# Masked cross-attention: values projected on 64-column tiles, chunk 0's mask loaded straight beside its queries, VectorE's first masks and value blocks placed elsewhere, the last chunks' steps in another order

## The reference

```python
Q = split_heads(x @ w_q.T + b_q)            # x: 4 x 1024 x 256
K = split_heads(ctx @ w_k.T + b_k)          # ctx: 4 x 64 x 256
V = split_heads(ctx @ w_v.T + b_v)
scores = Q @ K.T / 4                        # 4 x 16 x 1024 x 64
scores = where(mask[:, None] == 0, -1e9, scores)
attn = softmax(scores, axis=-1)
out = merge_heads(attn @ V) @ w_o.T + b_o + x
out = (out - mean) * rsqrt(var + 1e-5) * gamma + beta
```

## Time and profile before

| | us |
|---|---|
| median of 3 runs | 165.19 (164.49 to 167.47) |
| profiled execution, its own time | 164.33 |
| its span (first to last instruction) | 162.5 |
| PE busy | 137.3 (84%) |
| DVE busy | 124.9 (77%) |
| POOL busy | 115.5 (71%) |
| ACT busy | 94.7 (58%) |

### The profile page before, as it was taken

The page is one execution under the profiler, slowest core; times in us unless marked ns, Lnnn a source line. Parts: engine busy times, 40 slices in busy tenths (PEclk is TensorE's granted clock), DMA queues, the critical chain, the costliest instruction groups (busy, mean ns, idle before and its releaser), DMA issues.

```text
span 162.5 us, 2904 instructions
## 1 busy us (share of the span) xinstructions
PE 137.3 (84%) x992; PEld 87.0 (54%) x992; DVE 124.9 (77%) x231; ACT 94.7 (58%) x166; POOL 115.5 (71%) x111
## 2 busy tenths in 40 slices
PE   0798975989899998999899989998999579999400
PEld 0676853746556655565556565655665335468300
DVE  0263899348788897989798979898989797999951
ACT  3349687593963666766676675846763815640220
POOL 5003741029999539999999999999981899667783
PEclk9999999699999999999999999999999999999955
DMA  4988983999927886006730940048003503003024
GB/s 119 342 234 198 283 197 85 317 244 269 287 71 187 314 217 252 0 0 196 180 148 0 224 167 0 2 105 274 12 2 76 187 0 129 0 4 122 7 94 166
DMA packets 10175, 23.21 MB, mean 143 GB/s; under 512 B 1584, under 2 KB 1840, under 8 KB 10160
## 3 DMA queue, kind: packets, MB, share of 16 engines
q1 hardware_dynamic: 9584, 22.03, 46.7%
q10 hardware_dynamic: 576, 0.99, 1.9%
HBM read 14.62 MB, written 4.19 MB: 116 GB/s over the span
## 4 chain that ended last, share of the span: by engine, by line
PE 45%; DVE 15%; POOL 14%; issue 7%; DMA 7%; SPq 6%; ACT 3%; POOLq 1%; DVEq 0%
PE ps_w L436 11%; PE ps_w L357 9%; PE ps_w L331 8%; DMA m_sb<-maskT 7%; PE ps_s L385 6%; PE ps_s L412 5%; POOL y L873 5%; DVE nmax L667 4%; POOL y L876 4%; DVE turned L688 3%; SPq L215 3%; PE ps_s L391 3%; ACT y L585 2%; DVE cn L701 2%; POOL rstd L857 2%
## 5 line engine op out<-in xcount | busy, mean ns | idle before, releaser
L667 DVE TENSOR_REDUCE nmax<-ps_w 128x8 f32<-128x512 f32 x56 | 37.7, 678 | 15.2 <-PE ps_w L357 14.8
L572 ACT ACTIVATE probs<-ps_s 128x512 f32<-128x512 f32 x64 | 33.1, 602 | 18.3 <-PE ps_s L396 18.3
L810 POOL TENSOR_TENSOR xt_l<-xt_sb,xt_h 128x1024 fp32r<-128x1024 f32 x7 | 16.6, 2374 | 30.6 <-ACT xt_h L533 19.8
L436 PE MATMUL ps_w<-wo_sb,cn 128*128 128x256 f32 x112 | 29.3, 387 | 3.9 <-DVE cn L701 3.6
L357 PEld LDWEIGHTS ps_w<-k_half,q_mask 128*128 128x128 f32 x112 | 17.3, 190 | 25.5 <-DVE nmax L667 19.7
L357 PE MATMUL ps_w<-k_half,q_mask 128*128 128x256 f32 x112 | 27.9, 335 | 3.2 <-DVE nmax L667 2.9
L436 PEld LDWEIGHTS ps_w<-wo_sb,cn 128*128 128x128 f32 x112 | 19.3, 189 | 9.2 <-DVE cn L701 5.5
L585 ACT ACTIVATE y<-res,shift,rstd 128x256 f32<-128x256 f32 x28 | 14.8, 590 | 12.6 <-POOL shift L859 12.5
L873 POOL TENSOR_TENSOR y<-y,brow 128x512 f32<-128x512 f32 x14 | 17.9, 1279 | 4.5 <-ACT y L585 4.1
L688 DVE STREAM_TRANSPOSE turned<-ps_s 128x1024 f32<-128x1024 f32 x16 | 19.8, 1240 | 0.8 <-PE ps_s L412 0.8
L844 POOL TENSOR_TENSOR x_sb<-x_sb,brow 128x1024 f32<-128x1024 f32 x8 | 19.1, 2382 | 0.1
(11 more groups left out here) (75 smaller groups left out, 203.3 us busy)
## 6 DMA issues: line engine op xcount, KB each, us to landing
m_sb<-maskT SPq DMA_DIRECT2D x32, 128.0 KB, 3.5
q_mask<-mask SPq DMA_DIRECT2D x32, 128.0 KB, 2.6
x_sb<-x SPq DMA_DIRECT2D x8, 512.0 KB, 4.3
xt_sb<-xT SPq DMA_DIRECT2D x7, 512.0 KB, 4.4
out<-y SPq DMA_DIRECT2D x6, 512.0 KB, 3.4
xt_sb<-xT SPq DMA_DIRECT2D x2, 256.0 KB, 5.7
out<-xt_sb SPq DMA_DIRECT2D x2, 256.0 KB, 2.0
brow<-bias_rows SPq DMA_DIRECT2D x1, 384.0 KB, 6.4
```

Source lines behind the costliest of these rows:

```text
L436: return pe.matmul(tile_outputs(c, i)[:, t], cn[:, c % 2, j, (2 * i + t) * P:(2 * i + t + 1) * P], wo_sb[:, j], start=j == 0 and c < LAST, ...
L572: act.activation(probs[:, g % 2, quad], ps_s[:, quad], ACT.Exp).then_inc(e_done, 1)
L667: dve.tensor_reduce(nmax[:, c % 2, t].rearrange("p (q r) -> p q r", r=32)[:, :, 2 * j:2 * j + 2], max_bank(c, i).rearrange("p (q h k) -> p ...
```

## The change

Six things.

1. Values: `project_values` is one function. For each batch and each part of the width it makes two matmuls, one for the even and one for the odd heads, each with 64 stationary columns (the keys of one batch) and 128 moving ones (every other group of 16 columns of wv), into rows 0 to 63 or 64 to 127. ctx_t loses its fifth block. `value_blocks` has two instructions in place of five.
2. Chunk 0's mask: SyncE loads it twice more as int32 into `m_first`, rows 0 to 63 and 64 to 127, right after xT 0, and VectorE writes its values straight into `q_mask` (`first_mask_values`). The copies of mask 0 are gone; mask 0 in its usual form is loaded later, behind xT 1 and wv, and computed after the half keys.
3. VectorE's mask 2 and the value blocks stand after the third maximum of chunk 1, no longer after the eighth of chunk 0.
4. ScalarE takes the high part of chunk 1 before the first queries leave.
5. In step 6 the eighth maximum of chunk 7 stands before the moments of chunk 5. In the tail VectorE has `divide(6, 1)` after the residual and moments of chunk 5, TensorE `values(6, 1)` after the two outputs of chunk 5.
6. GpSimd has `last_deviations(0)` before the deviations of chunk 6's second half; the counts in `deviations_done` follow.

```diff
         def deviations_done(c, second):
-            return 4 * (c + 1) if c < LAST - 2 else 4 * (LAST - 2) + 4 * (2 * (c - LAST + 2) + second + 1)
+            if c < LAST - 2:
+                return 4 * (c + 1)
+            halves = 2 * (c - LAST + 2) + second + 1
+            return 4 * (LAST - 2) + (4 * halves if halves < 4 else 18 if c < LAST else 14 + 6 * second)
@@ sync
             load_first_xt(1)
+            for half in range(2):
+                sp.dma_start(m_first[rows(half)], maskT[0]).then_inc(in_mfirst, 16)
+            load_xt(1)
+            sp.dma_start(wv_sb[:], wv).then_inc(in_wv, 16)
             load_mask(0)
-            sp.dma_start(wv_sb[:], wv).then_inc(in_wv, 16)
-            load_xt(1)
-            copy_mask(0)
             load_mask(1)
@@ tensor
+            def project_values():
+                pe.wait_ge(in_wv, 16)
+                for b in range(BATCHES):
+                    for d in range(PC):
+                        for h in range(2):
+                            mm = pe.matmul(projected_values(h)[:, b], ctx_t[:, d, b],
+                                           wv_sb[:, d].rearrange("p (q e) -> p q e", e=32)[:, :, 16 * h:16 * h + 16],
+                                           start=d == 0, stop=d == PC - 1)
+                            if d == PC - 1:
+                                mm.then_inc(v_done, 1)
@@ max_scores
                 if i == 0:
-                    pe.wait_ge(mk_in[c % 2], 16 * QUADS * (c // 2 + 1))
+                    if c == 0:
+                        pe.wait_ge(mfirst_done, 2)
+                    else:
+                        pe.wait_ge(mk_in[c % 2], 16 * QUADS * (c // 2 + c % 2))
@@ tensor's list
             project_first_queries()
-            project_values(0)
-            project_values(1)
-            project_values(2)
+            project_values()
             max_scores(0, 0)
-            project_values(3)
             max_scores(0, 1)
...
                 if s == LAST:
-                    values(LAST - 1, 1)
                     output(LAST - 2, 1, 0)
                     output(LAST - 2, 1, 1)
+                    values(LAST - 1, 1)
                     scores(LAST, 1)
@@ scalar's list
             identity_rows(0)
+            high_x(1)
             first_queries_out(0)
-            high_x(1)
             first_queries_out(1)
@@ vector
+            def first_mask_values():
+                dve.wait_ge(in_mfirst, 32)
+                for half in range(2):
+                    r = rows(1 - half)
+                    dve.tensor_scalar(q_mask[r, 0, half], m_first[r].unsqueeze(1).to_broadcast([64, 2, CHUNK]), 0.0, -BIG,
+                                      ALU.is_equal, ALU.mult).then_inc(mfirst_done, 1)
...
             first_low_x()
-            mask_values(0)
+            first_mask_values()
...
             first_half_keys()
+            mask_values(0)
             for i in range(HALVES):
                 maxima(0, i)
                 if i == 3:
                     mask_values(1)
-            mask_values(2)
-            value_blocks()
             for s in range(LAST):
...
                 maxima(front, 2)
                 if s >= 2:
                     moments(s - 2, 1)
+                elif s == 0:
+                    mask_values(2)
+                    value_blocks()
                 maxima(front, 3)
...
                 maxima(front, 6)
-                if s >= 1:
+                if front == LAST:
+                    maxima(front, 7)
                     moments(s - 1, 0)
-                maxima(front, 7)
+                else:
+                    if s >= 1:
+                        moments(s - 1, 0)
+                    maxima(front, 7)
                 divide(s, 0)
-            divide(LAST - 1, 1)
             residual(LAST - 2, 1)
             moments(LAST - 2, 1)
+            divide(LAST - 1, 1)
             divide(LAST, 0)
@@ gpsimd's tail
             affine(LAST - 1, 0)
+            last_deviations(0)
             deviations(LAST - 1, slice(2, 4))
-            last_deviations(0)
             last_deviations(1)
```

More of the change, by code:

```diff
@@ L56, in build @@
         brow = sb("brow", [P, 4, D])
-        ctx_t = sb("ctx_t", [P, PC, BATCHES + 1, KEYS])
+        ctx_t = sb("ctx_t", [P, PC, BATCHES, KEYS])
         wq_sb = sb("wq_sb", [P, PC, D])
@@ L81, in build @@
         mask = sb("mask", [P, NM, 2, CHUNK], F32R)
+        m_first = sb("m_first", [P, CHUNK], I32)
         q_sb = sb("q_sb", [P, NQ, 2, CHUNK])
@@ L110, in build @@
         in_first = [sem(f"in_first{d}") for d in range(PC)]
-        in_bv = sem("in_bv")
+        in_bv, in_mfirst, mfirst_done = sem("in_bv"), sem("in_mfirst"), sem("mfirst_done")
         in_xt = [sem(f"in_xt{i}") for i in range(2)]
@@ L159, in max_bank, with projected_values @@
             return ps_s[:, 2 + i % 2] if c == 0 else ps_w[:, 0] if beside(c, i) else ps_w[:, 1]
-        def value_bank(b):
-            return (ps_c, ps_d)[b // 2]
+        def projected_values(h):
+            return (ps_c, ps_d)[h][rows(h), 0].rearrange("k (b p e) -> k b p e", b=BATCHES, e=16)
         def values_banks(g):
@@ L289, in project_keys @@
                         mm = pe.matmul(ps_w[:, 1, j * 256:j * 256 + 256], wk_sb[:, d, j * P:(j + 1) * P],
-                                       ctx_t[:, d, 0:BATCHES], start=d == 0, stop=d == PC - 1)
+                                       ctx_t[:, d], start=d == 0, stop=d == PC - 1)
                 mm.then_inc(k_done, 1)
[L293 to L301, removed]
+            def project_values():
[8 more added lines that the diff above has]
+                                mm.then_inc(v_done, 1)
             def project_first_queries():
@@ L402, in values @@
                 if g == 0:
-                    pe.wait_ge(vbd_done, 5)
+                    pe.wait_ge(vbd_done, 2)
                     pe.wait_ge(fill_done, 5)
@@ L671, in value_blocks @@
             def value_blocks():
-                dve.wait_ge(v_done, BATCHES)
+                dve.wait_ge(v_done, 2 * BATCHES)
                 dve.wait_ge(fill_done, 5)
                 dve.wait_ge(in_bv, 16)
-                for h, b, n, first in ((0, 0, 2, 0), (0, 2, 2, 2), (1, 0, 2, 1), (1, 2, 1, 3), (1, 3, 1, 0)):
+                for h in range(2):
                     r, e = rows(h), slice(16 * h, 16 * h + 16)
                     dve.tensor_tensor(
-                        v_bd[r, first:first + n, :, e],
-                        value_bank(b)[r, 0].rearrange("k (b p e) -> k b p e", b=2, e=32)[:, b % 2:b % 2 + n, :, e],
+                        v_bd[r, :, :, e], projected_values(h),
                         brow[r, 0].rearrange("k (p e) -> k p e", e=32)[:, :, e].unsqueeze(1)
-                        .to_broadcast([64, n, PAIRS, 16]), ALU.add).then_inc(vbd_done, 1)
+                        .to_broadcast([64, BATCHES, PAIRS, 16]), ALU.add).then_inc(vbd_done, 1)
             def divide(c, j):
@@ L736, in scaled @@
                 c = LAST
-                dve.wait_ge(ln_done, deviations_done(LAST - 1, True) + 2 * (i + 1))
+                dve.wait_ge(ln_done, deviations_done(c, i == 1))
                 dve.wait_ge(beta_done, 1)
@@ L866, in last_deviations @@
                 pool.tensor_scalar(veps[:, i, two], mv[:, i, two, 1], EPS, 1.0, ALU.add, ALU.mult).then_inc(ln_done, 1)
-                pool.wait_ge(ln_done, deviations_done(c - 1, True) + 2 * k + 1)
+                pool.wait_ge(ln_done, deviations_done(c, k == 1) - 1)
                 pool.tensor_tensor(rstd[:, i, two], veps[:, i, two], half_neg[:, two], ALU.pow).then_inc(ln_done, 1)
@@ L958 @@
         "ctxT": np.ascontiguousarray(
-            ctx[[*range(BATCHES), 0]].transpose(2, 0, 1).reshape(PC, P, BATCHES + 1, KEYS).transpose(1, 0, 2, 3)),
+            ctx.transpose(2, 0, 1).reshape(PC, P, BATCHES, KEYS).transpose(1, 0, 2, 3)),
         "wq": weight(L0_xattn_w_q), "wk": weight(L0_xattn_w_k),
```

## The result

| kernel | median | runs shown | ratio to before (95%) |
|---|---|---|---|
| before | 165.34 us | 164.49 to 167.47 | |
| after | 170.3 us | 169.34 to 172.28 | 1.0298 (1.0186 to 1.041) |

The change makes the kernel slower by 3.0%. The profiled execution of after took 169.44 us (span 167.6) against 164.33 (span 162.5): 5.1 us more. I had forecast 167.9, with a range to 169.3; the time lies above it.

The account below looks back on a forecast made before the run. TensorE's nearly unbroken chain from 45 to about 120 us shifts as a block, so its start and the tail decide. Mask 2.5, clock 1.0 and tail 0.1 add 3.6 to 164.33: 167.9 us, range 165.3 to 169.3.

Parts of the forecast that it names:

- g: Start, up to chunk 1's projection and `max_scores(1, 0)`: gain taken as 0.5 us, with cases of 0.7, none and 1.4.
- D: Chunk 2's mask on VectorE: done 2.5 us later, bounds 1.6 and 3.0, making `max_scores(2, 0)` +2.5 us.
- visible cost: VectorE held at chunk 2's mask, value blocks behind it, TensorE idle for the maxima; removing it looks like 3 us gain.
- GpSimd first and VectorE held until 16.0: Start, `low_x(1)` against chunk 0's full mask: VectorE begins the maxima at 16.6, so no gain.
- the upper end of my bounds: Delay of chunk 2's mask: 3.0 us, if tiles run one after the other and a hold leaves no start gain.
- +1.0, bounds 0 and 1.6: TensorE's clock after `max_scores(2, 0)`: one stretch at the lower level costs 1.0 us.
- The 3.6 us of the forecast: Whole kernel: total loss from 2.5 (chunk 2's mask), 1.0 (clock) and 0.1 (tail).
- +0.1, bounds 0 and 0.5: Tail: the last `affine` at 157.5 in place of 157.41, GpSimd setting the end.
- half a microsecond of cover: Tail: moments of chunk 6's first half end about 147.9, before GpSimd's 148.38; were cover gone, each tenth would be paid.
- (a): Rival at `max_scores(2, 0)`: the start's gain is kept, TensorE carries its 3.3 us through, 161.1 us; 7%.
- (b): Rival at start and clock: no hold at 13.6, mask delay 1.6, clock stays up, 165.3 to 166.3 us; 18%.
- (c): Rival at the start: tiles not side by side or VectorE held early, no start gain, clock low; 169.2 us; 13%.

Follow-up runs that it names:

- experiment 2: After, with SyncE's order changed alone: constant rows behind b_v's row, xT 3 ahead of the copies of mask 1; 163.31 us, ratio 0.9835.
- experiment 5: Before, with only chunk 2's mask and the value blocks put after chunk 1's third maximum; 171.0 us, ratio 1.0343.
- experiment 1: After, with chunk 2's mask alone back before chunk 1's maxima, value blocks still late; 167.21 us, ratio 1.0107.
- experiment 6: Before, with only the tail's new order on TensorE, VectorE and GpSimd; 166.07 us in ten runs, ratio 1.0021.
- experiment 7: Experiment 2 with the tail of before; 161.03 us, ratio 0.9742.
- experiment 11: After, with unused matmuls filling two TensorE pauses: four before `scores(1, 0)`, ten before `max_scores(2, 0)`; 167.96 us in ten runs, ratio 1.0123.
- experiment 12: Experiment 11 with six more unused matmuls before `output(5, 0)` in the tail; 168.35 us, ratio 1.0181.
- experiment 10: After, with ten unused matmuls of 512 columns before `max_scores(2, 0)` only; 171.46 us, ratio 1.0323.
- experiment 3: Before, with constant rows and xT 3 moved ahead on SyncE, before the copies of mask 1; 167.68 us, ratio 1.0164.
- experiment 9: Experiment 8 with xT 3 loaded ahead of mask 2 on SyncE as well; 162.37 us, ratio 0.9807.
- experiment 8: Experiment 7 with chunk 0's full mask put behind chunk 0's fourth maximum on VectorE; 165.69 us in ten runs, ratio 1.0039.
- experiment 4: Before, with constant rows and xT 3 between the load of mask 2 and the copies of masks 1 and 2; 167.66 us, four runs, no interval.

## Why the prediction was wrong

**The start: the places held, and g by luck.** The forecast put mask 2's end at 28.0 (27.74), the rows' issue at 31.7 (31.44), GpSimd's subtraction at 38.1 (37.95), `max_scores(2, 0)` at 43.0 (42.82), 2.0 us for the projection (1.97) and 0.5 for g (0.58). D was 2.3 for 2.5. Experiments 2 and 5 show the mechanism from both sides: the late mask alone loses 3.4%; the late mask with nothing needed behind it loses nothing. What I read as the visible cost, VectorE's hold of 2.4 us, was indeed worth nothing to take away there.

But g came out right by luck. The case that came, GpSimd first and VectorE held until 16.0 (16.02), is the one that I had priced at no gain, and it brought none; inputs that were there 0.64 us sooner made up for it. Reckoned from the end of that low part, `max_scores(2, 0)` comes 2.9 us later in after (42.82 - 8.76 against 40.53 - 9.40), and 3.0 in experiment 5, whose low part ended at 9.22. That is the upper end of my bounds.

**The hold.** VectorE was held at chunk 0's mask too: it ended 0.56 us after GpSimd did, as in the earlier trace rows. It goes both ways: GpSimd's `k_pair` took 2.49 us beside VectorE's mask, 2.04 before. The Trainium skill ("SBUF — State Buffer", SBUF: two separate sides) calls it an exclusive lock for a whole instruction; the rows agree.

**The clock: the step that failed.** "I take +1.0, bounds 0 and 1.6" had two faults. The bound came from a single low stretch of the earlier trace rows, 2.9 us long. Behind `max_scores(2, 0)` the fall cost 1.1 us in after, 2.0 in experiment 1 and 2.6 in experiment 5, where the low level lasted about 6 us. And I counted one fall. In the profiled execution a second one, in the tail, cost about 1.5 us (11.10 from `scores(6, 1)` to `scores(7, 0)`, against 9.59 with the same order and no fall in experiment 6). It stood in no term of the sum: the tail had +0.1, bounds 0 and 0.5, and measured 1.8. The 3.6 us of the forecast and these 1.5 are the 5.1 of the profiled execution.

I had no term for a fall at the start either. The change makes a pause of TensorE there, 2.50 us in after and 2.0 to 2.8 in all seven profiles in which VectorE computes chunk 0's full mask behind the half keys. In five of the seven (experiments 1, 2, 7, 11 and 12) the clock fell behind it, and `scores(0, 0)` came 15.4 to 15.7 us after the end of the low part, against 14.1 in after and 14.3 in experiment 10: 1.1 to 1.6 us more. The other seven profiles have no pause above 1.2 us and no fall there.

Of the 4.9 us that the ratio gives (0.0298 x 165.34), filling the two pauses ahead of chunk 1 brings back 2.1 us by the medians and 2.9 by the ratios, where I had taken 1.0 for the clock.

**The tail.** I took +0.1, with half a microsecond of cover at the moments of chunk 6's first half. The order alone costs +0.25 in the profile of experiment 6, inside my bounds, but not where I put it: GpSimd waits 0.23 us at `last_deviations(0)`, in experiment 6 (153.62) and in after alike, and the step I had watched, the moments of chunk 6's first half, brings no wait unless TensorE is late. In after it was, through the second fall, and there GpSimd waited 1.02 us at 153.21.

**The rivals.** (a) failed for the reason given: rows and mask 2 came later, not sooner. (b) needed D = 1.6 and a clock that stays up; no run has both. Experiment 11, whose clock stayed up from 21.4 us on, comes nearest and lies at 1.0123. (c) came nearest by its size of 169.2, and in part by its mechanism. The tiles did run side by side, but the other way that it names came true: VectorE was held early (13.29 to 16.02), the new start won nothing, and the clock fell. My range ended where (c) did, with one fall priced at 1.6.

**What stays open.** Why the clock falls in one execution of a kernel and not in the next. The tail's fall stands in the profiles of after and of experiments 1, 7 and 10, and not in those of before and the other nine. That is three of seven with the new tail order and one of seven with the old, too few to say whether the order has a part in it. It came behind a pause of 1.83 us before `output(5, 0)` that before has too (up to 128.75; up to 132.11 in after), as have experiments 2, 7 and 11, so that the pause alone does not decide it. Experiments 6 and 7 hint that the new order costs more than 0.25 us in some executions. By how much the falls at the start and in the tail move the median of after was not measured.

## What to carry to other kernels

Before an engine's work is moved into its idle time, follow what its semaphore releases, above all the DMA queue: here a mask that nobody needed for 15 us held xT 3 and the constant rows behind it. Before a load is moved ahead in the queue, look at what it passes: the same new order was worth 0.9835 on after and 1.0164 on before. A pause of TensorE can be paid twice, once as idle time and once as low clock; give the second a range of up to 2.6 us for each fall, the most seen here, and count the places where it can happen. Before a marker's shift is credited to a change, check when the inputs were there.

## What was unexpected in the hardware

- The low level lasted from 3.4 us (131.9 to 135.3 in after) over about 6.5 us (41.0 to 47.5 in experiment 1) to 10 us (27.2 to 37.2 in experiment 3). The longest single pause just ahead of it was 5.52 us in experiment 3 and 1.04 us in experiment 9 (up to 25.24), while behind a pause of 2.50 us (after, up to 16.67) the clock stayed at 1.00.
- Ten matmuls of 512 columns took 4.63 us at the lower level (experiment 10) and 2.57 us at the upper (experiment 11), the ratio being 1.80 and not 2.
- A copy of mask 1 (128 KB each) queued behind xT 3 (512 KB) and other loads kept TensorE waiting 3.6 to 5.5 us (experiments 8, 4 and 3), where it had waited 0.37.
